# Gated linear attention on one core: the half sums as four products side by side, turned by two full transposes

## The reference, cut to what matters

```python
g = jnp.cumsum(gc, axis=1)            # log decay summed within the chunk
g_last = g[:, -1]                     # its sum over the 64 tokens
qg = qc * jnp.exp(g); kg = kc * jnp.exp(-g)
A = jnp.einsum('cthd,cshd->chts', qg, kg)
A = A * jnp.tril(jnp.ones((C, C), q.dtype))
o_intra = jnp.einsum('chts,cshe->cthe', A, vc)
k_out = kc * jnp.exp(g_last[:, None] - g)
chunk_kv = jnp.einsum('cthd,cthe->chde', k_out, vc)
decay = jnp.exp(g_last)
def step(S, inp):
    kv, dec, qg_c = inp
    o_inter = jnp.einsum('thd,hde->the', qg_c, S)
    return (S * dec[..., None] + kv, o_inter)
```

## Time and profile before

| | us |
|---|---|
| median of 3 runs | 2974.84 |
| lowest and highest run | 2967.43 and 2976.77 |
| span of the profiled execution | 2973.1 |
| PE busy in it | 2792.8 (94%) |
| DVE busy | 2498.2 (84%) |
| ACT busy | 2081.2 (70%) |
| POOL busy | 881.3 (30%) |

### The profile page before, as it was taken

How to read it: one execution, slowest core, us unless ns; L and a number is a source line. 1 busy time by engine, 2 the same in 40 slices (tenths; PEclk the granted TensorE clock), 3 DMA queues, 4 the chain that set the end, 5 groups by cost and what they waited for, 6 DMA issues and landing times.

```text
span 2973.1 us, 58047 instructions
## 1 busy us (share of the span) xinstructions
PE 2792.8 (94%) x23085; PEld 1251.6 (42%) x23085; DVE 2498.2 (84%) x3270; ACT 2081.2 (70%) x3906; POOL 881.3 (30%) x1050
## 2 busy tenths in 40 slices
PE   8999999999999989999999999999888799978889
PEld 2222222235666632222222356666333265467755
DVE  8999999976777689999999767776799956899854
ACT  6999999975666569999999766665777423735232
POOL 1000000012343310000000123433388655199810
PEclk9999999999999999999999999999999999989999
DMA  2000000000000010000000000000000000000000
GB/s 94 7 16 18 17 18 16 14 8 1 2 1 2 2 54 6 17 16 17 17 17 15 12 1 1 1 2 2 27 1 0 10 1 1 0 1 1 1 1 15
DMA packets 29148, 33.62 MB, mean 11 GB/s; under 512 B 13195, under 2 KB 23438, under 8 KB 28622
## 3 DMA queue, kind: packets, MB, share of 16 engines
q1 hardware_dynamic: 28878, 29.92, 3.5%
HBM read 17.58 MB, written 7.34 MB: 8 GB/s over the span
## 4 chain that ended last, share of the span: by engine, by line
PE 68%; DVE 19%; ACT 6%; issue 3%; POOL 2%; DMA 0%; SPq 0%; DVEq 0%; POOLq 0%; PEldq 0%; ACTq 0%
PE banks L401 15%; PE banks L383 10%; DVE max_parts L528 7%; PE banks L376 5%; PE banks L1114 3%; PE banks L2147 2%; PE banks L1025 2%; PE banks L2132 2%; PE banks L2134 2%; PE banks L1088 2%; PE banks L1133 2%; PE banks L1057 2%; ACT probs L644 2%; DVE banks L2998 2%; DVE state_keys L2995 2%
## 5 line engine op out<-in xcount | busy, mean ns | idle before, releaser
L528 DVE TENSOR_REDUCE max_parts<-banks 128x2 f32<-128x1024 f32 x1024 | 1170.7, 1217 | 11.5 <-PE banks L376 9.9
L644 ACT ACTIVATE probs<-banks 128x512 f32<-128x512 f32 x2048 | 1085.3, 599 | 59.8 <-PE banks L383 33.2
L383 PE MATMUL banks<-q_parts,k_parts 51*128 51x512 bf16 x2048 | 654.6, 385 | 4.8 <-ACT v_heads L603 1.5
L401 PE MATMUL banks<-probs,v_heads 128*9 128x256 f32 x8192 | 637.7, 383 | 8.2 <-ACT pv_copy L655 2.0
L376 PE MATMUL banks<-k_parts,q_parts 48*128 48x512 bf16 x2048 | 595.5, 385 | 10.5 <-DVE max_parts L528 6.0
L383 PEld LDWEIGHTS banks<-q_parts,k_parts 51*128 51x128 bf16 x2048 | 151.8, 94 | 474.7 <-ACT probs L644 397.1
L711 POOL CAST neg_max_parts<-neg_max 128x8 bf16<-128x8 f32 x64 | 13.0, 203 | 1122.5 <-DVE neg_max L533 1122.5
L401 PEld LDWEIGHTS banks<-probs,v_heads 128*9 128x9 f32 x8192 | 123.4, 88 | 382.0 <-issue 343.0
L1681 POOL TENSOR_TENSOR state_times_c<-state,c_row 128x1024 f32<-128x1024 f32 x63 | 148.0, 2354 | 88.8 <-ACT c_row L1997 54.2
L1875 DVE TENSOR_TENSOR_SCAN state<-banks,state_carry,state 128x512 f32<-128x512 f32 x128 | 157.3, 1271 | 6.4 <-ACT banks L1992 4.3
L2318 ACT ACTIVATE silu_a<-banks 128x512 f32<-128x512 f32 x80 | 47.7, 597 | 163.0 <-PE banks L2132 162.8
(11 more groups left out here) (526 smaller groups left out, 5053.3 us busy)
## 6 DMA issues: line engine op xcount, KB each, us to landing
outT_half<-pv_copy SPq DMA_DIRECT2D x248, 16.0 KB
prob_sums<-pv_copy SPq DMA_DIRECT2D x248, 2.0 KB
q_scratch<-qk_parts SPq DMA_DIRECT2D x8, 384.0 KB, 2.5
k_scratch<-qk_parts SPq DMA_DIRECT2D x8, 384.0 KB, 2.6
k_parts<-k_scratch SPq DMA_DIRECT2D x28, 96.0 KB
q_parts<-q_scratch SPq DMA_DIRECT2D x28, 96.0 KB
q_parts<-neg_max_rows SPq DMA_DIRECT2D x128, 3.0 KB
ffn_weights<-moe SPq DMA_DIRECT2D x1, 1928.0 KB, 7.6
```

The source lines that it names most:

```text
L383: nc.tensor.matmul(bank("exp", n, x)[:, :], K[p % 2][half_of(x, ROWS + PARTS), tile(t)], Q[p % 2][half_of(x, ROWS + PARTS), blk(j)], start ...
L401: i = nc.tensor.matmul(PVb[group:group + VD, cols], V[:, t + k, 2 * (s // NB) + x, :], PT[:, (n + k) % RING, x, cols], start=(t == 0 and c ...
L528: nc.vector.tensor_reduce(mxp[s % 2][:, :, u // NB, u % NB], Mb[m % 2].rearrange("p (x k) -> p x k", x=2), AX.X, ALU.max).then_inc(*maxed. ...
L644: nc.scalar.activation(PT[:, n % RING, x, :], bank("exp", n, x)[:, :], ACT.Exp, scale=float(HD) ** -0.5).then_inc(*exped.inc())
```

## The change

`halves` makes four products where there were two: each mask is now multiplied with the even and with the odd blocks of 128 channels apart (r = 0, 1), 256 moving columns each, and the four results stand in partitions 0 to 31, 32 to 63, 64 to 95 and 96 to 127 of the same bank, 256 columns wide. `exp_half` reads and writes 128 x 256 where it was 64 x 512. `turn_halves` makes two transposes of 128 x 128 where there were four of 64 x 128. What stands in `Dbank` afterwards is in the same places as before, so `state_decay` is the same.

```diff
-        eh_rows = sb("exp_half_rows", [64, KD])
+        eh_rows = sb("exp_half_rows", [128, KD // 2])
...
+        every_other = lambda ap, r: ap.rearrange("p (c r y) -> p r c y", r=2, y=128)[:, r, :, :]
...
             def halves(t):
                 pe.wait_ge(*bank_read("rows", t))
                 pe.wait_ge(masks_begun, 3)
-                nc.tensor.matmul(bank("rows", t)[0:32, :], half_dense[:, :, :].rearrange("p s x -> p (s x)"), gk[t % 2][:, 0, :], start=True, stop=True)
-                nc.tensor.matmul(bank("rows", t)[32:64, :], half[:, t, :, :].rearrange("p s x -> p (s x)"), gk[t % 2][:, 1, :], start=True, stop=True).then_inc(*halves_made.inc())
+                for r in range(2):
+                    for k, lhs in ((0, half_dense[:, :, :]), (1, half[:, t, :, :])):
+                        i = nc.tensor.matmul(bank("rows", t)[64 * r + 32 * k:64 * r + 32 * k + 32, 0:KD // 2], lhs.rearrange("p s x -> p (s x)"),
+                                             every_other(gk[t % 2][:, k, :], r), start=True, stop=True)
+                i.then_inc(*halves_made.inc())
...
             def turn_halves(t):
...
-                for r in range(4):
-                    i = nc.tensor.transpose(Dbank[:, 256 + 64 * r:320 + 64 * r], eh_rows[:, tile(r)], g.ident[0:64, 0:64])
+                for c in range(2):
+                    i = nc.tensor.transpose(Dbank[:, 256 + 128 * c:384 + 128 * c], eh_rows[:, tile(c)], g.ident[:, :])
                 i.then_inc(*halves_turned.inc())
...
             def exp_half(t):
                 act.wait_ge(halves_made, t + 1)
                 act.wait_ge(halves_turned, t)
-                nc.scalar.activation(eh_rows[:, :], bank("rows", t)[0:64, :], ACT.Exp, scale=1 / 16.0).then_inc(*halves_exped.inc())
+                nc.scalar.activation(eh_rows[:, :], bank("rows", t)[:, 0:KD // 2], ACT.Exp, scale=1 / 16.0).then_inc(*halves_exped.inc())
```

## The result

| | before | changed |
|---|---|---|
| median, us | 2974.32 (2967.43 to 2976.77, 4 runs) | 2954.81 (2952.71 to 2959.56, 4 runs) |
| ratio | | 0.9944, 95% interval 0.9929 to 0.9960 |
| profiled execution, span | 2973.1 | 2955.0 (time of that run 2956.39) |

The changed kernel is faster by 0.56% by the ratio; the interval is 12 to 21 us. The two medians lie 19.5 us apart. 2958 was forecast. A second set of five runs on another occasion gave 0.9939 (0.9926 to 0.9953).

What follows compares the result with a forecast made beforehand. PE was taken to bound the GLA loops; 13.2 (half sums), 2.2 (turning), 0.6 (entries) and 0.5 (first rounds) make 16.5 us, 2973.1 to 2956.6. With the median 1.7 above the span, forecast 2958 us, range 2948 to 2969.

Steps and rivals of the forecast that it cites:

- PE bounds the loop, its time comes through in full: In both GLA loops, a microsecond less on PE is one less per round, unless another engine has less slack.
- Part 1: Half sums on PE: four products side by side take 0.55 us instead of 0.99, saving 0.44 per tile.
- I take that at nothing: Half sums: reading the moving operand in two pieces of 128 with a hole between them costs nothing.
- Part 2: Turning on PE: two transposes for four make 0.92 us into 0.84, saving 0.08 per tile; bounds 0.01 lost to 0.17 saved.
- Part 3: Exponential on ACT: 0.595 us becomes about 0.374; worth nothing in the loop, on the path before it.
- Part 4: Ends and entries: last turning gives nothing, entries 0.30 us per call, slow first rounds 0.4 and 0.1 extra.
- The last turning of a call does not count: End of each call: the chain goes over ACT and DVE to POOL's `state_middle`, so PE's saving is waited away.
- 1: Half sums: only two column groups run at once, so they still cost 0.99 us; 2972 us in all; chance 6%.
- 2: DVE's slack behind `q_experts`, or the operand's hole, loses half the gain, 6.6 us; 2965 us; chance 9%.
- rival 3: Half sums: the four products run one after the other, 1.85 us, 0.86 more than before; 2998 us; chance 2%.
- The sum: Half sums 13.2, turning 2.2, entries 0.6, slow first rounds 0.5: together 16.5 us saved.

Runs made afterwards that it cites:

- halves_twice: Changed kernel with the four products of the half sums issued a second time, same operands and place; round 21.48 us against 21.05.
- turn_twice: Changed kernel with its two transposes in `turn_halves` issued a second time, same operands and place; round 21.27 us against 21.05.
- contiguous: Changed kernel with 256 channels in a row as moving operand, the hole moved to the transposes' output; round 21.05 us, as in the changed kernel.
- turn_moved: Kernel before, its four transposes of 64 rows moved on PE from before `update_dense` to behind `project`; round 21.71 us against 21.64.
- exp_twice: Changed kernel with the exponential of the half sums taken twice on ACT; round 21.05 us, as in the changed kernel.
- two_groups: Kernel before with four products of 256 columns, but only in its two column groups, so two at a time; round 21.64 us, as before.

## Why the prediction was right

- **PE bounds the loop, its time comes through in full.** Right: in the ordinary round 0.59 less on PE is 0.59 less in the round, and `halves_twice` (+0.43) and `turn_twice` (+0.22) came through as well. It failed in one round per call, the third, where DVE's routing takes the slack, in part because it is held up behind POOL: 0.5 us each. The prediction took the slack of DVE from an ordinary round and did not look at that one.
- **Part 1, the half sums.** 0.55 expected, 0.57 measured, 0.42 saved for 0.44. The price was taken from L401, which leaves 0.12 to its next line beside its 0.43 of columns; the passage here is 0.14. "I take that at nothing" of the hole in the operand is shown by `contiguous`.
- **Part 2, the turning: the mis-sized term.** 0.08 per tile was taken, 0.17 measured, the upper bound. The step that failed is the reading "so 0.21 are columns and 0.18 is the passage to L1141's shape", and with it "I take the 0.18 that led there before". The single starts show that only 0.10 of the 0.18 is passage. It is 0.10 from L1039's shape and 0.10 from 128 x 128, in the changed kernel and in `turn_moved`, and `turn_twice` shows that it comes once. The other 0.08 lay among L1039's own four transposes, 0.05 of it behind the first one, and went with them. The 0.09 into 64 rows that goes was right. The Trainium skill, "TensorEngine Tiling (Array Packing)", section "Tiling Modes", has the drain at each change of mode. The runs agree, with 0.09 to 0.10 in front of each change at the turning, and add 0.05 behind L1039's first transpose.
- **Part 3.** Right: `exp_twice`. The exponential itself takes 0.418, not 0.374.
- **Part 4.** In part wrong, in part open. "The last turning of a call does not count" is wrong: from `sum_squares` in front of it to the last `x_added` the traces have 21.58 and 21.59 before and 21.41 in both calls now, so its 0.17 comes through. In the entry, the chain from `exp_half` to the first ACT copy behind the turning went from 1.62 to 1.24 in the first call, 0.38 for the 0.30 booked. `halves(1)` there went from 1.85 to 1.01, but the clock granted over the first 10 us of the loop was 0.68 before and 0.83 after, so what is the change's share stays open. The first rounds gave 2.0 and 0.6 us in the two traces (31.09 to 29.10, 29.75 to 29.16), but `two_groups`, where nothing should change, had 29.75 and 28.11. Entries and first rounds move by up to 3 us from run to run, and the 1.1 us booked for them can't be shown.
- **Rivals.** 1 is refuted by the four rows that begin within 0.02, and `two_groups` shows what it would have cost. 2 named the right place (DVE's slack), which was thinned to 0.42 but held, except in the third round; DVE's 128 x 2048 product took 2.27 beside the four streams and 2.28 before, so the two do not hold each other up. 3 is refuted by the same rows as 1. The Trainium skill, "TensorE: Matmul & The Clock Gate", section "The mechanism", lets a load overlap matmuls in flight only when the row group differs. It also names the background weight buffer, and no run here tells whether these loads go there. Here four more loads begin at 857.44 to 857.46 on the same 128 rows, 0.01 to 0.03 behind the fourth matmul (857.43) and 0.2 before the fifth, so the measurement decides against rival 3.
- **The sum.** 28 later rounds were to give 28 x 0.52 = 14.6 us; by their rounds they gave 7.7 per call, 15.5 together: more by the turning, less by the third rounds. The measured ratio 0.9944 is 16.7 us on 2974.32; 16.5 had been forecast. That close an agreement is partly luck: 0.09 more per turning and 0.5 lost in each third round pull against each other, the interval of the ratio is 12 to 21 us, and the medians themselves differ by 19.5.

## What to carry to other kernels

Price a product by the moving columns of its column group and by the change of shape around it, not by its number of instructions: with four groups of 32 columns at once the half sums' columns took 0.43 us, with two at once 0.86. A transpose of the same shape as its neighbours saves a change of shape. Before a passage is priced as a remainder, look at the single starts: here 0.08 of a remainder of 0.18 belonged to the group itself. Look at the odd rounds (where routing or a late block stands) and not only at the regular one for slack. After a saving on the bounding engine look at who frees the banks it writes next: here the following 0.11 was given back in full until one copy changed engines or came earlier.

## What the runs showed that was not expected

- Four transposes of 64 columns cost 0.08 us more than their columns and the passage behind them: 0.05 behind the first one after the change of shape, the rest spread over the others. The passage into 128 rows x 64 columns was 0.10 from either shape.
- Sixteen records of 128 columns in four groups took the same 0.57 us as eight of 256.
- Moving instructions to a cheaper place on the bounding engine made the round longer (21.71 for 21.64), and 0.22 of that were waits on copies by ACT that had 0.17 us to spare.
- A product of 128 x 48 on DVE took 0.38 to 1.78 us, and ended 0.06 after the POOL product that ran beside it, wherever that began.
